# Two layer norms shared between VectorE and ScalarE, and a clamp with a second tensor in place of a constant

## The chip, the cores and the metric

The kernel runs on one NeuronCore of one Trainium2 chip. The metric is the device time of one execution in microseconds (us). The kernel before takes 867.91 us, the median of 3 runs (865.51 to 868.33).

## What is computed

Activations of 16 sequences of 256 tokens with 128 features (4096 tokens) pass through four sublayers, each on a layer norm of its input and added back to it. Cut to what matters here:

```
ln(x)   = (x - mean(x)) / sqrt(var(x) + 1e-5)                # over the 128 features
x = x + mixing(ln(x));  x = x + moe(ln(x))
x = x + attention(ln(x));  x = x + moe(ln(x))

mixing(x): Q = l2norm(x @ W_q.T); K = l2norm(x @ W_k.T); V = x @ W_v.T
           return Q * mean over the sequence of (K * V)
l2norm(t) = t / max(norm(t), 1e-12)
moe(x):    a shared 128-512-128 MLP, plus the top 2 of 8 experts of the same shape
```

The change touches the norm ahead of the mixing, the mixing's `max(norm, 1e-12)`, and the norm ahead of the first mixture of experts.

## The kernel before, in words

The tokens lie in `xres` as 32 tiles of 128 tokens (partitions) by 128 features in f32. A batch b is two tiles (one sequence); a group g is four batches, that is 8 tiles, and there are four groups. Each engine has its own instruction stream, written out by hand, and waits on semaphores.

**The first two norms** are `norm(r)`, r = 0 (ahead of the mixing) and r = 1 (ahead of the experts). VectorE merges the statistics, ScalarE takes the square root (`std`, line 1384), VectorE the reciprocal (line 1715). Then, a group at a time:
- the rows: `xn = (xres - mean) * rstd`, 8 instructions of 128x128 a group on VectorE (line 1720, `norm_rows`), mean and rstd being one value a partition
- `hi` on ScalarE (line 1391): the f16 part of the group's 128x1024 elements, into `hl`
- `lo` on VectorE (line 1727): what hi leaves over, one 128x1024 instruction that reads `xn` and `hl`
- TensorE turns both parts of each batch (line 894, four transposes) into one of four PSUM banks; when a bank has been copied out it is free for the batch four later
- the copies to `xT`: ScalarE has 12 batches (line 1395: 0 to 8, 10, 12, 14), VectorE has 9, 11, 13, 15 (line 1732), after its last `lo`

VectorE's order is rows 0, rows 1, lo 0, rows 2, lo 1, rows 3, lo 2, lo 3, copies. ScalarE's is hi 0, hi 1, copies of group 0, hi 2, copies of group 1, hi 3, the rest. In norm(1) TensorE adds the gate's eight small matmuls a batch (line 877, 128x8) when a batch is copied, and GpSimd adds each group of `xn` into `xres` (line 722) once that group's `hi` is done. The route, which VectorE works out, waits for the last gate logits.

**GpSimd meanwhile** scales and splits the weights of 8 experts and of the shared MLP (lines 690 to 698, operations of 128x512 that read SBUF), as SyncE's loads bring them, from norm(0) into the mixing; then it fills `place16` and `vx` by MEMSET (lines 707, 708) and copies into `place16` (line 712).

**Between norm(0) and the mixing** VectorE splits the biases and the transposed weights (lines 2333 to 2355); the mixing's first projection waits for that.

**The mixing** runs over the 16 batches, two PSUM banks a batch, with VectorE one batch ahead in part. For a batch TensorE projects (6 matmuls of 384 columns), ScalarE squares and sums (line 1411, four with their accumulator reads), takes the root (line 1417) and copies (line 1420). On VectorE a step is: clamp of batch b+1 (line 1748, 128x4 elements), half of `back` (line 1766), reciprocal (line 1753), the other half, `front` of b+1 (line 1759, two), statistics of b-1 (line 1694, two), the add into `xres` (line 1771, 128x256, reads two SBUF tensors).

**After norm(1)** TensorE starts the shared MLP (lines 877 and 1036) while VectorE routes.

Of the kernel before, what the change touches and what calls it, by code (L numbers as in the profile page):

```python
# [34 lines left out]
def build(nc, x, W_q, W_k, W_v, qkv_w, qkv_b, out_w, out_b, gate_w, gate_b, sh_w1, sh_b1, sh_w2,  # L35
# [50 lines left out]
    with ctx:  # L86
        def sb(name, shape, dt):
            return ctx.enter_context(nc.sbuf_tensor(name, shape, dt))

        def sem(name):  # L90
            return ctx.enter_context(nc.semaphore(name))
# [46 lines left out]
        var = sb("var", [P, T], F32)  # L138
        gap = sb("gap", [P, T], F32)
        rstd = sb("rstd", [P, T], F32)  # L140
        bnat = sb("bnat", [P, 56], F32)
        bhi = sb("bhi", [P, 56], F16)
        blo = sb("blo", [P, 56], F16)
# [137 lines left out]
        class Ln:  # L281
            stats = sem("ln_stats")
            var = sem("ln_var")
            merge = sem("ln_merge")
            std = sem("ln_std")
            rstd = sem("ln_rstd")
            norm = sem("ln_norm")
            hi = sem("ln_hi")
# [349 lines left out]
        def _(pool):  # L638
# [21 lines left out]
            pool.memset(cXS[:, :], XS)  # L660
            pool.memset(zero16[:, :], 0.0)
            pool.memset(cWS[:, :], WS)
            pool.memset(epsx[:, :], 1e-5 / (XS * XS))
            link(pool.memset(eps[:, :], 1e-5))
            for m in (ident16, ident32):
# [714 lines left out]
        def _(act):  # L1380
            def std(r):
                l, first = Ln, r * NBATCH
                act.wait_ge(l.var, r + 1)
                act.activation(rstd[:, :], var[:, :], ACT.Sqrt, bias=eps[:, 0:1], scale=1.0 / D).then_inc(l.std, 1)

            def norm(r):
                l, first = Ln, r * NBATCH

                def hi(g):
                    act.wait_ge(l.norm, NG * r + g + 1)  # L1390
                    act.activation(group(hl, g)[:, :, 0:D], group(xn, g), ACT.Copy, scale=XS).then_inc(l.hi, 1)

                def copy_out(b):
                    act.wait_ge(l.turned, first + b + 1)
                    act.activation(two(xT, b), LB[b % GB][:, 0:4 * P].rearrange("p (c f) -> p c f", c=CB),
                                   ACT.Copy).then_inc(l.xT, 1)

                for g in range(NG):
                    hi(g)
                    if 0 < g < NG - 1:  # L1400
                        for b in range(GB * (g - 1), GB * g):
                            copy_out(b)
                for b in SBATCH[2 * GB:]:
                    copy_out(b)

# [280 lines left out]
        def _(dve):  # L1686
# [14 lines left out]
            def norm(r):  # L1701
                l, first = Ln, r * NBATCH


                dve.wait_ge(l.stats, (r + 1) * NBATCH)
                dve.tensor_tensor(mean[:, :], stats[:, :, 1], stats[:, :, 4], ALU.add)
                dve.tensor_tensor(var[:, :], stats[:, :, 2], stats[:, :, 5], ALU.add)
                dve.tensor_tensor(gap[:, :], stats[:, :, 1], stats[:, :, 4], ALU.subtract).then_inc(l.merge, 1)
                dve.wait_ge(l.merge, 2 * r + 1)
                dve.tensor_scalar(mean[:, :], mean[:, :], 0.5, None, ALU.mult)  # L1710
                dve.tensor_tensor(gap[:, :], gap[:, :], gap[:, :], ALU.mult).then_inc(l.merge, 1)
                dve.wait_ge(l.merge, 2 * r + 2)
                dve.scalar_tensor_tensor(var[:, :], gap[:, :], D / 4.0, var[:, :], ALU.mult, ALU.add).then_inc(l.var, 1)
                dve.wait_ge(l.std, r + 1)
                dve.reciprocal(rstd[:, :], rstd[:, :]).then_inc(l.rstd, 1)
                dve.wait_ge(l.rstd, r + 1)

                def norm_rows(g):
                    for t in range(GT * g, GT * (g + 1)):
                        last = dve.tensor_scalar(xn[:, t, :], xres[:, t, :], mean[:, t:t + 1], rstd[:, t:t + 1],  # L1720
                                                 ALU.subtract, ALU.mult)
                    last.then_inc(l.norm, 1)

                def lo(g):
                    dve.wait_ge(l.hi, NG * r + g + 1)
                    h = group(hl, g)
                    dve.scalar_tensor_tensor(h[:, :, D:2 * D], group(xn, g), XS, h[:, :, 0:D],  # L1727
                                             ALU.mult, ALU.subtract).then_inc(l.lo, 1)

                def copy_out(b):  # L1730
                    dve.wait_ge(l.turned, first + b + 1)
                    dve.tensor_copy(two(xT, b), LB[b % GB][:, 0:4 * P].rearrange("p (c f) -> p c f", c=CB))\
                        .then_inc(l.xTv, 1)

                norm_rows(0)
                norm_rows(1)
                for g in range(2, NG):
                    lo(g - 2)
                    norm_rows(g)
                lo(NG - 2)  # L1740
                lo(NG - 1)
                for b in VBATCH:
                    copy_out(b)

            def mix():
                def clamp(b, u):
                    dve.wait_ge(Mix.std, b + 1)
                    dve.tensor_scalar(rnorm[:, u, :, :], rnorm[:, u, :, :], PS * 1e-12, None, ALU.max)\  # L1748
                        .then_inc(Mix.clamped, 1)

                def invert(b, u):
# [635 lines left out]
```

## Time and profile before

| | before |
|---|---|
| median of 3 runs | 867.91 us (865.51 to 868.33) |
| the profiled execution, its own time | 864.54 us |
| span of the profile | 862.7 us |
| TensorE matmul busy | 685.2 us (79%) |
| VectorE busy | 646.9 us (75%) |
| ScalarE busy | 526.3 us (61%) |
| GpSimd busy | 478.7 us (55%) |
| mean granted TensorE clock | 0.91 of full speed |

The shares are means over all stages. By the chain of work that ended last TensorE carries 57% of the span and VectorE 25%; among the lines of that chain are 1720 (the rows of the first two norms, 4%), 1748 (the clamp, 1%) and 1727 (`lo`, 1%). A stage's bound is read from that chain in order of time, and then from the timeline of each engine in that stretch. In the timeline a row is `start, duration, engine, line, operation, out<-in, shape, count`; a row with a count above 1 covers that many instructions from the first's start to the last's end. Instructions of one engine overlap a little at their ends, so the distance from start to start is shorter than the duration of one.

### The profile page before, as it was taken

How to read it: one execution, taken by the hardware profiler on the slowest of the kernel's cores; microseconds unless marked ns; L12 is line 12 of the kernel's file. 1: busy time of each engine (PE TensorE's matmuls, PEld its weight loads, DVE VectorE, ACT ScalarE, POOL GpSimd, SP SyncE). 2: the span in 40 equal slices, each digit the busy share in tenths (PEclk: the TensorE clock that was granted, in tenths of full speed). 3: DMA queues.
4: the chain of work that ended last, by engine and by line, in shares of the span. 5: the costliest groups of instructions: out<-in, count | busy, mean ns of one | idle time of the engine just before them, and what ended most of it. 6: DMA issues, size and time to landing. Idle time of an engine off the chain costs nothing.

```text
span 862.7 us, 22793 instructions
## 1 busy us (share of the span) xinstructions
PE 685.2 (79%) x7807; PEld 488.3 (57%) x7808; DVE 646.9 (75%) x1433; ACT 526.3 (61%) x1236; POOL 478.7 (55%) x496
## 2 busy tenths in 40 slices
PE   1265289699999906889989989997989949999980
PEld 1233289588898903334434444443438939888980
DVE  7979969477777443889989888987766228888748
ACT  3366364276676504588889788877775526666640
POOL 3987315677876277848227206003577737777740
PEclk9999569899999955699989998998899969999995
DMA  7222110033335111101000000000011322333236
GB/s 193 73 74 31 46 54 2 25 78 88 91 85 79 47 49 46 32 8 35 17 2 2 2 1 2 2 2 2 21 53 57 108 58 74 86 82 90 74 106 198
DMA packets 62745, 46.88 MB, mean 54 GB/s; under 512 B 8771, under 2 KB 57067, under 8 KB 62680
## 3 DMA queue, kind: packets, MB, share of 16 engines
q1 hardware_dynamic: 53592, 28.02, 12.1%
q0 software_dynamic: 9088, 17.98, 8.2%
q8 instruction: 42, 0.69, 0.3%
q14 instruction: 23, 0.19, 0.1%
HBM read 26.76 MB, written 20.13 MB: 54 GB/s over the span
## 4 chain that ended last, share of the span: by engine, by line
PE 57%; DVE 25%; ACT 6%; issue 5%; POOL 5%; DMA 2%; SPq 0%; DVEq 0%; ACTq 0%; POOLq 0%
PE ps L877 30%; PE ps L1021 12%; DVE mx L2226 6%; PE ps L1255 5%; DVE xn L1720 4%; PE ps L1036 3%; POOL rows L827 3%; DVE xres L2123 2%; PE ps L1113 2%; POOL gy L756 2%; PE ps L1268 1%; ACT scratch L1590 1%; DVE rnorm L1748 1%; DVE hlo L2219 1%; DVE hl L1727 1%
## 5 line engine op out<-in xcount | busy, mean ns | idle before, releaser
L1466 ACT ACTIVATE h<-ps,b1T 128x256 f32<-128x256 f32 x440 | 171.9, 479 | 56.8 <-PE ps L877 56.8
L2226 DVE TENSOR_REDUCE mx<-ps 128x2 f32<-128x512 f32 x256 | 171.9, 687 | 30.6 <-PE ps L877 29.1
L1590 ACT ACTIVATE scratch<-ps 128x512 f32<-128x512 f32 x256 | 149.4, 603 | 37.7 <-PE ps L877 36.3
L877 PE MATMUL ps<-xg,w1s 128*128 128x256 f16 x936 | 117.9, 277 | 11.4 <-issue 9.5
L1021 PE MATMUL ps<-w2s,hhi 128*128 x1248 | 117.3, 219 | 0.0
L838 POOL DMA_INDIRECT ytok<-yst,didx x78 | 89.5, 1148 | 42.9 <-DVE yst L2057 22.2
L877 PE MATMUL ps<-kst,qst 32*128 32x256 f16 x512 | 97.5, 290 | 10.6 <-DVE mx L2226 10.3
L742 POOL DMA_INDIRECT scratch<-rows,tok_i x78 | 89.9, 1153 | 26.8 <-issue 23.2
L1492 ACT ACTIVATE xg<-ps 128x512 f16<-128x512 f16 x78 | 46.5, 597 | 95.1 <-PE ps L1113 95.1
L877 PEld LDWEIGHTS ps<-xg,w1s 128*128 x936 | 88.5, 99 | 25.7 <-issue 15.5
L1999 DVE SCALAR_TENSOR_TENSOR hlo<-h,hhi 128x1024 f16<-128x1024 f32 x78 | 95.6, 1225 | 2.7
L877 PE MATMUL ps<-hlo,kst 32*128 32x256 f16 x512 | 94.5, 282 | 3.2 <-ACT scratch L1590 2.8
L1021 PEld LDWEIGHTS ps<-w2s,hhi 128*128 128x128 f16 x1248 | 86.3, 98 | 0.2
L1021 PE MATMUL ps<-w2s,hlo 128*128 x624 | 85.9, 219 | 0.0
L1255 PE MATMUL ps<-scratch,vx 128*32 128x256 f32 x1024 | 84.3, 403 | 0.3 <-ACT scratch L1590 0.3
L756 POOL DMA_INDIRECT gy<-ysorted,slot_i x64 | 61.9, 967 | 39.0 <-DMA ysorted<-yst 20.2
L827 POOL DMA_INDIRECT rows<-hl,slot_i x64 | 62.6, 978 | 19.4 <-issue 18.9
L1997 DVE TENSOR_SCALAR hhi<-h 128x1024 f16<-128x1024 f32 x78 | 54.7, 701 | 23.8 <-ACT h L1466 20.5
L1036 PE MATMUL ps<-w2f,h 128*128 128x128 f32 x512 | 63.0, 277 | 0.5 <-ACT h L1466 0.5
L773 POOL TENSOR_SCALAR yst<-xres,mean,rstd 128x128 f32<-128x128 f32 x24 | 18.7, 787 | 80.3 <-DVE rstd L2189 80.3
L2057 DVE SCALAR_TENSOR_TENSOR yst<-ps,b2s 128x256 f32<-128x256 f32 x78 | 33.1, 425 | 38.1 <-PE ps L1021 38.0
L1036 PEld LDWEIGHTS ps<-w2f,h 128*128 128x128 f32 x512 | 59.7, 192 | 1.0 <-ACT h L1466 0.7
(310 smaller groups left out, 1345.7 us busy)
## 6 DMA issues: line engine op xcount, KB each, us to landing
gy<-rows SPq DMA_DIRECT2D x39, 136.0 KB, 2.2
ysorted<-yst SPq DMA_DIRECT2D x39, 128.0 KB, 1.9
h<-in_L_ffn_ew SPq DMA_DIRECT2D x16, 256.0 KB, 3.1
scratch<-ytok SPq DMA_DIRECT2D x16, 256.0 KB, 3.4
xres<-in_L_attn_a_x SPq DMA_DIRECT2D x4, 512.0 KB, 6.1
rows<-hl SPq DMA_DIRECT2D x4, 512.0 KB, 3.3
out_x<-xres SPq DMA_DIRECT2D x4, 512.0 KB, 4.3
scratch<-rows,tok_i POOLq DMA_INDIRECT x78, 2.8
```

Of the source, the lines that this page charges most:

```text
L742: pool.indirect_dma_start(grow[:, BT * (f % 4) + t, :], None, rows_dram, bass.IndirectOffsetOnAxis(ap=tok_i[:, n:n + 1], axis=0))\
L756: pool.indirect_dma_start(gy[:, f % 4, TOPK * c + k, :], None, y_dram, bass.IndirectOffsetOnAxis(ap=slot_i[:, k, t:t + 1], axis=0))\
L827: pool.indirect_dma_start(region_dram, bass.IndirectOffsetOnAxis(ap=slot_i[:, k, t:t + 1], axis=0), hl[:, t, :], None).then_inc(Post.sent, 16)
L838: pool.indirect_dma_start(ytok_dram, bass.IndirectOffsetOnAxis(ap=didx[:, u, t:t + 1], axis=0), yst[:, u, t, :], None, bounds_check=most, ...
L877: return pe.matmul(o, a, b, start=start, stop=stop)
L1021: last = pe.matmul(YB[u % 2][:, t, :], h[:, u % 2, at:at + P], w, start=(c, k, t) == (0, 0, 0), stop=(c, k, t) == (CH - 1, 2, BT - 1), ski ...
L1036: pe.matmul(YB[q % 2][:, t, :], h32[:, q % 2, at:at + P], w2f[:, c * D:(c + 1) * D], start=(c, t) == (0, 0), stop=False, skip_group_check= ...
L1255: last = pe.matmul(ps[32 * hh:32 * hh + 32, 4 + jp, n * SEQ:(n + 1) * SEQ], vx[:, u, kc, 4 * (2 * jp + n) + hh, :], prb[:, (4 * g + hh) % ...
L1466: last = act.activation(h32[:, u % 2, f], HB[u % 2][:, f], ACT.Gelu_apprx_tanh, bias=b1T[:, ds(e * CH + c, 1)], scale=1.0 / PS)
L1590: act.activation(prb[:, (s // 4 * 4 + (s + 2) % 4) % 8, :], ps[:, s % 2, :], ACT.Exp, scale=HD ** -0.5 / (PS * PS))\
L1999: dve.scalar_tensor_tensor(hlo[:, u, :], h32[:, u, :], XS, hhi[:, u, :], ALU.mult, ALU.subtract)\
L2226: dve.tensor_reduce(mx[:, c, j:j + 5:4], ps[:, 2 + s % 2, :].rearrange("p (n k) -> p n k", n=2), AX_X, ALU.max).then_inc(Att.mx, 1)
```

## The change

In norm(0) and norm(1):
- VectorE makes one more small vector, `shift = -mean * rstd` (128x32).
- The rows of groups 1 and 3 move to ScalarE: `Identity(rstd * x + shift)`, 8 instructions a group, both operands one value a partition. ScalarE's order becomes rows 1, hi 0, hi 1, rows 3, hi 2, copies of group 0, hi 3, copies of group 1, the rest.
- The rows of groups 0 and 2 stay on VectorE, as SCALAR_TENSOR_TENSOR in place of TENSOR_SCALAR: `rstd` is given as a second tensor, one column read 128 times. VectorE's order becomes rows 0, rows 2, lo 0, lo 1, lo 2, lo 3, copies.
- The semaphore `std` becomes `by_act` and counts three steps a norm.

In the mixing the clamp reads its bound from a constant tensor `least` (128x2x2, filled once by GpSimd at the start) as TENSOR_TENSOR, in place of a constant in TENSOR_SCALAR.

```diff
@@ vector, norm(r)
-                dve.wait_ge(l.std, r + 1)
+                dve.wait_ge(l.by_act, 3 * r + 1)
                 dve.reciprocal(rstd[:, :], rstd[:, :]).then_inc(l.rstd, 1)
-                dve.wait_ge(l.rstd, r + 1)
+                dve.wait_ge(l.rstd, 2 * r + 1)
+                dve.scalar_tensor_tensor(shift[:, :], mean[:, :], -1.0, rstd[:, :], ALU.mult, ALU.mult)\
+                    .then_inc(l.rstd, 1)
 
                 def norm_rows(g):
                     for t in range(GT * g, GT * (g + 1)):
-                        last = dve.tensor_scalar(xn[:, t, :], xres[:, t, :], mean[:, t:t + 1], rstd[:, t:t + 1],
-                                                 ALU.subtract, ALU.mult)
+                        last = dve.scalar_tensor_tensor(xn[:, t, :], xres[:, t, :], mean[:, t:t + 1],
+                                                        rstd[:, t:t + 1].to_broadcast([P, D]),
+                                                        ALU.subtract, ALU.mult)
                     last.then_inc(l.norm, 1)
...
                 norm_rows(0)
-                norm_rows(1)
-                for g in range(2, NG):
-                    lo(g - 2)
-                    norm_rows(g)
-                lo(NG - 2)
-                lo(NG - 1)
+                norm_rows(2)
+                for g in range(NG):
+                    lo(g)
                 for b in VBATCH:
                     copy_out(b)
@@ vector, mix()
-                    dve.tensor_scalar(rnorm[:, u, :, :], rnorm[:, u, :, :], PS * 1e-12, None, ALU.max)\
+                    dve.tensor_tensor(rnorm[:, u, :, :], rnorm[:, u, :, :], least[:, :, :], ALU.max)\
                         .then_inc(Mix.clamped, 1)
@@ scalar, norm(r)
+                def scaled_rows(g):
+                    act.wait_ge(l.rstd, 2 * r + 2)
+                    for t in range(GT * g, GT * (g + 1)):
+                        last = act.activation(xn[:, t, :], xres[:, t, :], ACT.Identity, bias=shift[:, t:t + 1],
+                                              scale=rstd[:, t:t + 1])
+                    last.then_inc(l.by_act, 1)
+
                 def hi(g):
-                    act.wait_ge(l.norm, NG * r + g + 1)
+                    if g % 2:
+                        act.wait_ge(l.by_act, 3 * r + g // 2 + 2)
+                    else:
+                        act.wait_ge(l.norm, 2 * r + g // 2 + 1)
                     act.activation(group(hl, g)[:, :, 0:D], group(xn, g), ACT.Copy, scale=XS).then_inc(l.hi, 1)
...
-                for g in range(NG):
+                scaled_rows(1)
+                hi(0)
+                hi(1)
+                scaled_rows(3)
+                for g in range(2, NG):
                     hi(g)
-                    if 0 < g < NG - 1:
-                        for b in range(GB * (g - 1), GB * g):
-                            copy_out(b)
+                    for b in range(GB * (g - 2), GB * (g - 1)):
+                        copy_out(b)
```

## Rows read from the trace of the kernel before

**Rows 1.** Chain of waits in order of time, norm(0): start, us, what.
```profile
13.86 4.19 DVE xn L1720 x16
...
19.19 6.54 DVE xn L1720 x8
...
34.93 3.59 PE ps L894 x32
```

**Rows 2.** Chain of waits, from the mixing to the experts.
```profile
77.82 2.92 DVE rnorm L1748
...
92.77 6.29 DVE xn L1720 x16
...
110.78 0.59 PE ps L894 x4
...
115.84 5.71 PE ps L877 x64
```

**Rows 3.** Timeline of norm(0): GpSimd's first weights, and VectorE's `lo` among them.
```profile
18.92 2.16 POOL L690 TENSOR_TENSOR h<-h,cWS 128x512 f32<-128x512 f32 x2 [13.17 <-DMA h<-in_L_ffn_ew]
25.65 2.07 DVE L1727 SCALAR_TENSOR_TENSOR hl<-xn,hl 128x1024 f16<-128x1024 f32 x1
26.59 1.60 POOL L694 CAST w1s<-h 128x512 f32 x1
```

**Rows 4.** Timeline of ScalarE, norm(0) and later: what its row instruction is priced by.
```profile
15.44 0.23 ACT L1672 ACTIVATE gws<-scratch 128x8 f16<-128x8 f32 x1
16.04 1.06 ACT L1391 ACTIVATE hl<-xn 128x1024 f16<-128x1024 f32 x1 [0.36 <-DVE xn L1720]
19.89 2.06 ACT L1395 ACTIVATE xT<-ps 128x512 f16<-128x512 f16 x4 [0.74 <-PE ps L894]
92.03 0.32 ACT L1384 ACTIVATE rstd<-var,eps 128x32 f32<-128x32 f32 x1 [4.62 <-DVE var L1713]
115.86 1.28 ACT L1458 ACT_TABLE_LOAD   x1
201.04 1.56 ACT L1466 ACTIVATE h<-ps,b1T 128x256 f32<-128x256 f32 x4
```

**Rows 5.** Timeline: VectorE's STT of 128x128 from SBUF; a tiny two-tensor operation.
```profile
854.84 4.27 DVE L2123 SCALAR_TENSOR_TENSOR xres<-scratch,wtop,xres 128x128 f32<-128x128 f32 x15
128.44 0.17 DVE L1978 TENSOR_TENSOR e<-e,e 128x8 f32<-128x8 f32 x1
```

**Rows 6.** Timeline of the mixing: clamps and adds beside GpSimd.
```profile
53.07 0.41 DVE L1771 TENSOR_TENSOR xres<-xres,scratch 128x256 f32<-128x256 f32 x1
53.14 0.81 POOL L694 CAST w2s<-h 128x512 f32 x1
53.39 0.58 DVE L1748 TENSOR_SCALAR rnorm<-rnorm 128x4 f32<-128x4 f32 x1
77.16 1.80 POOL L707 MEMSET place<- 128x2048 f16 x1
82.33 0.29 DVE L1748 TENSOR_SCALAR rnorm<-rnorm 128x4 f32<-128x4 f32 x1
```

**Rows 7.** Two lines of VectorE, all instructions: duration ns least/median/most, first and last start.
```profile
L1748 DVE TENSOR_SCALAR rnorm<-rnorm x16: 155/575/2984, 46.3 to 87.0; 128x4 f32<-128x4 f32 x16
L1771 DVE TENSOR_TENSOR xres<-xres,scratch x16: 399/409/1048, 49.7 to 90.0; 128x256 f32 x12, 128x256 f32<-128x256 f32 x4
```

**Rows 8.** Timeline of norm(1): GpSimd's first and last add, and the `lo` beside it.
```profile
96.08 2.38 POOL L722 TENSOR_TENSOR xres<-xres,xn 128x1024 f32<-128x1024 f32 x1 [13.49 <-ACT hl L1391]
109.42 2.43 DVE L1727 SCALAR_TENSOR_TENSOR hl<-xn,hl 128x1024 f16<-128x1024 f32 x2
110.67 3.39 POOL L722 TENSOR_TENSOR xres<-xres,xn 128x1024 f32<-128x1024 f32 x1 [2.79 <-ACT hl L1391]
```

**Rows 9.** Stretches: length, busy PE, PEld, DVE, ACT, POOL, granted clock, DMA share, GB/s.
```profile
116.00:120.00 4.00, 4.00 (x50) 3.06 (x48) 3.18 (x8) 3.27 (x5) 0.00 (x0) 0.50 0.03 7
122.00:126.00 4.00, 4.00 (x40) 3.87 (x39) 1.95 (x4) 2.30 (x8) 0.00 (x0) 1.00 0.00 0
```

More of the change, by code:

```diff
@@ L140, in build @@
         rstd = sb("rstd", [P, T], F32)
+        shift = sb("shift", [P, T], F32)
+        least = sb("least", [P, CB, 2], F32)
         bnat = sb("bnat", [P, 56], F32)
@@ L284, in build @@
             merge = sem("ln_merge")
-            std = sem("ln_std")
+            by_act = sem("ln_by_act")
             rstd = sem("ln_rstd")
@@ L662, in _ @@
             pool.memset(cWS[:, :], WS)
+            pool.memset(least[:, :, :], PS * 1e-12)
             pool.memset(epsx[:, :], 1e-5 / (XS * XS))
@@ L1383, in std @@
                 act.wait_ge(l.var, r + 1)
-                act.activation(rstd[:, :], var[:, :], ACT.Sqrt, bias=eps[:, 0:1], scale=1.0 / D).then_inc(l.std, 1)
+                act.activation(rstd[:, :], var[:, :], ACT.Sqrt, bias=eps[:, 0:1], scale=1.0 / D).then_inc(l.by_act, 1)
             def norm(r):
                 l, first = Ln, r * NBATCH
+                def scaled_rows(g):
[4 more added lines that the diff above has]
+                    last.then_inc(l.by_act, 1)
                 def hi(g):
-                    act.wait_ge(l.norm, NG * r + g + 1)
+                    if g % 2:
+                        act.wait_ge(l.by_act, 3 * r + g // 2 + 2)
+                    else:
+                        act.wait_ge(l.norm, 2 * r + g // 2 + 1)
                     act.activation(group(hl, g)[:, :, 0:D], group(xn, g), ACT.Copy, scale=XS).then_inc(l.hi, 1)
```

## The prediction

> **What bounds the kernel now.** I read the chain of work that ended last in order of time, then each engine's timeline in the stretches that the change touches. In norm(0) the chain is VectorE's rows and `lo` from 13.86, then TensorE's turns from 34.93 to 38.52 [rows 1]. The reader should compare the row stretches: 16 rows take 4.19 us, but the 8 rows of group 2 take 6.54 [rows 1]. The difference is GpSimd, which starts on the weights at 18.92 [rows 3]. From then on VectorE and GpSimd take turns: `lo` starts at 25.65 and takes 2.07, where half of two later ones is 1.21 [rows 8], and GpSimd's cast, queued at 26.59, takes 1.60 because `lo` runs first [rows 3]. In the mixing, clamps of 128x4 elements take a median of 575 ns where the shortest takes 155 [rows 7]; one sits 2.92 us on the chain, just behind the start of GpSimd's MEMSETs [rows 2, 6]. norm(1) is bound by VectorE again, from 92.77 until TensorE's last unbroken run begins at 110.78; the stage ends at 115.84 [rows 2]. So all three places are on the path, and what is saved there moves everything behind it: the shared MLP on TensorE, and the route, which waits for the gate logits. The expert weights don't come in between: GpSimd is past them at 77.16 [rows 6], 38 us before they are used.
>
> **Prices.** (a) A row on VectorE as SCALAR_TENSOR_TENSOR: 15 of the same form (128x128, one pointer, two tensors in SBUF) take 4.27 us [rows 5], so they start about 0.28 us apart. The old form takes 4.19/16 = 0.26 [rows 1]. VectorE loses 0.02 a row on 32 rows and is rid of the other 32.
> (b) A row on ScalarE: no row of the trace has two pointers. From SBUF, 1024 elements take 1.06 and 32 elements with a pointer 0.32; four of 256 elements with a pointer take 1.56, so they are at most 0.39 apart [rows 4]. Half the elements take off 0.11 (0.83 ns each: 1.06 us less some 0.2 fixed, over 1024). A second pointer adds about 0.09: the 0.32 less 0.03 for its elements, less the 0.2. That gives 0.37; I take 0.375 apart. Bounds: 0.28 (as if pointers were free) and 0.49 (0.2 + 0.11 + two pointers, with no overlap).
> The Trainium skill, "ScalarE: Activation LUTs", section "What ACT_TABLE_LOAD costs", has 186 ns + 0.833 ns an element, about 93 ns for each pointer and an overlap of about 93 ns: an estimate of 0.386 apart, by which norm(0) would end 0.2 us later.
> (c) `shift` lies between 0.17 (128x8) and 0.28 (128x128) [rows 5]; 0.2 in norm(1). In norm(0) it is hidden behind ScalarE's weight copies, which end at 15.67 [rows 4].
> (d) The clamp with two tensors: 0.17 us by the nearest row [rows 5], against 0.155. What it waits for is the question. The add of line 1771 also has two tensors in SBUF: it takes 0.40 at least and up to 1.05 [rows 7]. So a two-tensor operation is held up too when GpSimd reads SBUF. At 53.07 the add goes first, GpSimd's cast queues behind it (to 53.95), and the next clamp queues behind the cast (0.58, to 53.97) [rows 6]. Nothing in that depends on the clamp's form. I take as gone only the wait behind the MEMSETs, which read nothing.
> The Trainium skill has this as a rule ("SBUF — State Buffer", "Who interferes with whom"): an instruction with two SBUF inputs contends with a GpSimd instruction that reads SBUF, not with one that only writes. The trace agrees for the add (up to 1.05); for a MEMSET beside a two-tensor operation it has no row. Against the change speaks "VectorE: DVE Perf Modes" of the skill: f32 TENSOR_SCALAR has twice the rate of a two-tensor form, an estimate of 32x128/0.96 GHz/2 = 2.1 us lost; the rows show 32x0.02 = 0.6.
>
> **norm(0), step by step.** VectorE: `shift`, then 16 rows from 14.0, done at 14.0+16x0.28 = 18.5, before GpSimd starts at 18.92 [rows 3]; no row is held up any more. ScalarE is now the bound. From 15.6: rows 1 take 8x0.375+0.1 = 3.1, to 18.7; hi 0 and hi 1, 0.95 apart, to 20.6; rows 3 to 23.6; hi 2 to 24.6; four copies (four take 2.06, [rows 4]) to 26.5; hi 3 to 27.45; four copies to 29.4. Beside it the four `lo` each wait for the GpSimd operation under way (0.6 to 1.1) and then take 1.14: done at about 21.1, 23.3, 26.7 and 29.0, none later than ScalarE needs it. The turns of batches 8 to 11 follow the copies of 4 to 7 (28.0 to 29.9), the last four follow the copies of 8 to 11, about 0.45 apart, and end at 31.8. Before they ended at 38.52 [rows 1]. Gain 6.7. At 0.28 or 0.49 a row the chain moves by 16 times the difference: 8.2 or 4.9.
> VectorE's splits of biases and weights follow; I leave their length as it was. GpSimd is held up about 1.1 us by each `lo`, four instead of three: it ends some 1.2 later, hidden by the 38 us above.
>
> **The mixing.** It starts 6.7 earlier, and GpSimd's weights end 1.2 later. The MEMSET wait of 2.8 goes. But beside GpSimd the clamps come (77.8-46.3)/12 = 2.62 us apart [rows 2, 7]; from there to the last, at 87.0 [rows 7], three steps take 9.2, or 6.4 without that wait. These now lie beside GpSimd's weights too: 3x2.62 = 7.9. Net gain 2.8-1.5 = 1.3; bounds 0 (the clamp waits for the MEMSETs all the same, or lands in other waits) and 2.8.
>
> **norm(1)**, in us from the first row; GpSimd is idle at first. VectorE's 16 rows end at 16x0.28+0.07 = 4.55. ScalarE's rows 1 end at 3.2, hi 0 at 4.2. That frees GpSimd's add of group 0 (2.38, [rows 8]) beside VectorE's last row, and lo 0. Before, hi 3 freed lo 3 and the last add together: `lo` went first and the add took 3.39 [rows 8]. From then on the two alternate, 1.15+2.4 = 3.55 a group: if lo 0 starts at 4.55, lo 3 ends at 4.55+3x3.55+1.15 = 16.35; if the add goes first, at about 18.7. Before, lo 3 ended at 109.42+2.43-92.77 = 19.1 [rows 8, 2], but what set the end, 115.84-92.77 = 23.1, was lo 2 and the eight turns with gates behind it, 5.06. Now it is lo 3 and four turns with gates: some 3.3, so 19.7 or 22.0. Gain 3.4 or 1.1.
> What is late next is TensorE's clock: it is granted 0.50 in 116 to 120 and 1.00 in 122 to 126 [rows 9], that is 1.2 and 2.4 GHz, after an unbroken run from 110.78. The new unbroken run begins only behind lo 3 (16.4 or 18.8, before 18.0), so some 2 us more of the MLP run at half speed: cost 1.0. Net 2.4 or 0.1. The ends of hi 0 and of VectorE's rows lie 0.35 apart, too near to call; I take 1.1.
>
> **Sum.** 6.7 + 1.3 + 1.1 = 9.1 us. The profiled execution would go from 864.54 to 855.4. It lies 3.4 below the median of the runs shown; the median would go from 867.91 to 858.8. All bounds low: 4.9+0+0.1 = 5.0; all high: 8.2+2.8+2.4 = 13.4. The runs before scatter by 1.4 around their middle.
>
> **Rivals.** 1. *Two-tensor operations are not held up by GpSimd's reads.* Then all clamps come as near as the last ones, (87.0-82.33)/2 = 2.33 [rows 6, 7]: 15x2.33 = 35.0 for 40.7, gain 5.7 in the mixing. norm(1) loses its alternation, follows ScalarE and ends near 17.6: 4.5 after the clock's cost. In all 6.7+5.7+4.5 = 16.9, 851.0. For it: the median add takes 0.409, though GpSimd is busy most of that time. Against: the 1.05. Chance 0.12.
> 2. *The waits for GpSimd fall badly*: its adds go first in norm(1), and four VectorE operations more on the path (splits, adds, `lo`) arrive just behind a GpSimd one and wait 1.0 each. Gain 6.7+0.1+1.3-4.0 = 4.1, 863.8; with more such waits down to 1. For it: at 96.08 the add took its plain 2.38 while VectorE was in its rows [rows 8], so it gets in between any two. Against: VectorE's rows no longer lie in GpSimd's way. Chance 0.14.
> 3. *ScalarE's rows are far dearer.* The place is ScalarE's queue in both norms; 0.1 us a row costs 1.6 in norm(0), and 1.6 in norm(1) once the 4.4 us are used up by which hi 3 (11.95) leads the end of lo 3. The 9.1 are gone at 0.375+(9.1+4.4)/32 = 0.80 a row; at 1.0 the kernel would be 6.4 slower, 874.3. A function table loaded (1.28, [rows 4]) at each change to Identity and back would cost up to six loads, 7.7 us: 866.5. Against: 256 elements with a pointer stay below 0.39 apart, and in the mixing Square, Sqrt and Copy alternate without a load. Chance 0.06, of it 0.04 slower than before.
> The Trainium skill ("ScalarE: Activation LUTs", "Table sets: the hidden batching unit") has copy and identity in every set; no row here has Identity.
>
> **How the numbers follow.** Forecast (gain 5.0 to 13.4) 0.68; rivals 0.12, 0.14, 0.06. The range takes in the forecast's bounds with the scatter (853.1 to 864.3) and so part of rival 2: 853.0 to 864.5. A measurement of this kernel can tell about 0.3%, 2.6 us, from no change. Faster by more: 0.91 (forecast, rival 1, most of rival 2); within: 0.05 (the rest of rival 2, rival 3's loads); slower: 0.04.
>
> **What would show it.** norm(0): no row of VectorE longer than 0.35; ScalarE without a gap from 15.6 to 29, its rows 0.375 apart; the last turn near 31.8, the mixing's first matmul near 36. Mixing: clamps still near 0.57 beside reading GpSimd, none near 2.9. norm(1): whether lo 0 or add 0 starts first, lo 3 ending 16.35 or 18.7 from the first row, the clock's rise 27 to 29 from it. Wrong would be: ScalarE's rows above 0.49, a table load between them, or clamps all near 0.17.

## The result, and the profile after

| | before | after |
|---|---|---|
| median, runs taken side by side | 868.12 us (865.51 to 868.59) | 857.37 us (854.40 to 857.90) |
| profiled execution, its span | 864.54, 862.7 | 857.65, 855.8 |

The ratio is 0.987, 95% interval 0.983 to 0.991: faster by 10.8 us between the medians, and the interval stands for 7.5 to 15 us. The two profiled executions lie only 6.9 apart; where the other 3.9 are is told below. The page of after:

```profile
span 855.8 us, 22796 instructions
PE 688.5 (80%) x7807; PEld 487.9 (57%) x7808; DVE 632.7 (74%) x1403; ACT 537.4 (63%) x1268; POOL 483.5 (56%) x497
PE 57%; DVE 21%; ACT 7%; POOL 6%; issue 5%; DMA 2%; SPq 1%; DVEq 0%; ACTq 0%; POOLq 0%
```

Four marks divide the part that the change touches: the end of the last turn of norm(0), the first matmul of the mixing, the reciprocal of norm(1), and matmul 390, one of the last 40 matmuls of the gates, just ahead of the shared MLP. From the same marks of both traces:

| us from the span's start | before | after | stage shorter by |
|---|---|---|---|
| last turn of norm(0) ends | 38.50 | 32.03 | 6.5 |
| mixing's first matmul | 42.78 | 37.03 | -0.7 |
| norm(1)'s reciprocal | 92.38 | 86.47 | 0.2 |
| matmul 390 | 115.84 | 105.00 | 4.9 |

The sum is 10.8, and 10.7 of it still stand at matmul 2470 (295.34 before, 284.64 after).

**norm(0)** in the chain of waits of after (start, us, what), where [rows 1] had VectorE's rows:

```profile
15.86 3.05 ACT xn L1395 x8
18.91 1.89 ACT hl L1404 x2
20.80 3.08 ACT xn L1395 x8
...
28.22 3.82 PE ps L897 x32
...
32.41 0.91 DVE bhi L2349
...
33.40 1.02 DVE blo L2353
...
34.48 0.94 DVE qkb L2359
```

ScalarE has taken VectorE's place on the chain. The last three lines are the splits of biases behind the norm: operations on three and two columns that take about 1 us each, because GpSimd holds them off (the first two end within 0.03 us of the end of one of its operations). In before the same three took 0.40, 0.91 and 1.01: two of them were held off there already. All instructions of the two row lines (duration ns least/median/most, first and last start):

```profile
L1395 ACT ACTIVATE xn<-xres,shift,rstd x32: 477/492/511, 15.7 to 94.8; 128x128 f32<-128x128 f32 x32
L1738 DVE SCALAR_TENSOR_TENSOR xn<-xres,mean,rstd x32: 343/344/348, 14.0 to 90.9; 128x128 f32<-128x128 f32 x32
```

**The mixing.** Clamps and adds of after, where [rows 7] had 155/575/2984 and 399/409/1048, and the clamp that met a MEMSET, where [rows 2] had 2.92:

```profile
L1764 DVE TENSOR_TENSOR rnorm<-rnorm,least x16: 151/562/1111, 40.6 to 81.0; 128x4 f32<-128x4 f32 x16
L1787 DVE TENSOR_TENSOR xres<-xres,scratch x16: 401/748/1236, 43.7 to 84.1; 128x256 f32 x12, 128x256 f32<-128x256 f32 x4
...
75.84 1.80 POOL L710 MEMSET place<- 128x2048 f16 x1
76.43 0.15 DVE L1764 TENSOR_TENSOR rnorm<-rnorm,least 128x4 f32<-128x4 f32 x1
```

The long wait is gone, the typical clamp is as slow as it was, and the adds have become slower (the median from 409 to 748 ns).

**norm(1)**: the timeline of VectorE and GpSimd in after, where [rows 8] had the last `lo` and the last add beside each other:

```profile
86.97 4.28 DVE L1738 SCALAR_TENSOR_TENSOR xn<-xres,mean,rstd 128x128 f32<-128x128 f32 x16
91.25 4.52 DVE L1746 SCALAR_TENSOR_TENSOR hl<-xn,hl 128x1024 f16<-128x1024 f32 x2
91.30 13.26 POOL L725 TENSOR_TENSOR xres<-xres,xn 128x1024 f32<-128x1024 f32 x4 [10.03 <-ACT hl L1404]
96.22 6.12 DVE L1746 SCALAR_TENSOR_TENSOR hl<-xn,hl 128x1024 f16<-128x1024 f32 x2 [0.46 <-ACT hl L1404]
```

`lo` 0 started 0.05 us ahead of the first add. From there the two take turns to 102.34. But in the chain of waits of the stage it is ScalarE's queue that leads, to the end of its last `hi`, and VectorE has only the last `lo` in it:

```profile
87.08 3.19 ACT xn L1395 x8
...
98.11 0.95 ACT hl L1404
99.09 3.27 DVE hl L1746
...
102.49 0.59 PE ps L897 x4
```

**Where 3.9 us went.** Behind matmul 2470 the profiled execution of after gives back what the medians keep. The stretches of before and then of after (length, busy PE, PEld, DVE, ACT, POOL, granted clock, DMA share, GB/s):

```profile
590.00:625.00 35.00, 32.16 (x342) 14.52 (x341) 25.76 (x60) 26.30 (x54) 17.43 (x25) 0.85 0.04 11
```

```profile
590.00:625.00 35.00, 34.52 (x354) 14.86 (x354) 25.21 (x57) 24.18 (x51) 19.08 (x26) 0.76 0.07 22
```

TensorE's clock is at 0.50 for 17.1 us from 590.0 in after, for 10.2 us from 598.8 in before. The lead falls there from 9.57 us (matmul 5200) to 7.07 (matmul 5590); another 1.2 went between matmuls 2470 and 3120, where after has one more stretch at 0.50, 3.4 us from 364.7. Nothing of the change lies there, and the profiled execution of before (864.54) was quicker than all four of its timed runs (865.51 and more), while that of after (857.65) was a typical one. So I put the 3.9 down to which executions were profiled; that is argued from these rows, not shown by a run.

### The profile page after: what moved, and what is told of

It is laid out like the page before. It is cut to its first block, busy times and chain, and to the rows that moved or that the text cites. A ratio compares the mean times of both kernels' runs of the same rounds, so it can differ in the third digit from the quotient of the medians.

```text
span 855.8 us, 22796 instructions
## 1 busy us (share of the span) xinstructions
PE 688.5 (80%) x7807; PEld 487.9 (57%) x7808; DVE 632.7 (74%) x1403; ACT 537.4 (63%) x1268; POOL 483.5 (56%) x497
## 3 DMA queue, kind: packets, MB, share of 16 engines
q0 software_dynamic: 9088, 17.98, 8.3%
## 4 chain that ended last, share of the span: by engine, by line
PE 57%; DVE 21%; ACT 7%; POOL 6%; issue 5%; DMA 2%; SPq 1%; DVEq 0%; ACTq 0%; POOLq 0%
PE ps L880 30%; PE ps L1024 12%; DVE mx L2242 6%; PE ps L1258 6%; PE ps L1039 3%; POOL rows L830 3%; DVE xres L2139 2%; PE ps L1116 2%; POOL gy L759 2%; PE ps L1271 2%; ACT xn L1395 1%; DVE hlo L2235 1%; DVE rnorm L1764 1%; DVE xres L1787 1%; ACT hl L1404 1%
## 5 line engine op out<-in xcount | busy, mean ns | idle before, releaser
L745 POOL DMA_INDIRECT scratch<-rows,tok_i x78 | 91.7, 1175 | 26.8 <-issue 19.8
L1258 PE MATMUL ps<-scratch,vx 128*32 128x256 f32 x1024 | 86.8, 413 | 0.3 <-ACT scratch L1606 0.3
```

The costliest lines, as they stand in the source:

```text
L745: pool.indirect_dma_start(grow[:, BT * (f % 4) + t, :], None, rows_dram, bass.IndirectOffsetOnAxis(ap=tok_i[:, n:n + 1], axis=0))\
L1258: last = pe.matmul(ps[32 * hh:32 * hh + 32, 4 + jp, n * SEQ:(n + 1) * SEQ], vx[:, u, kc, 4 * (2 * jp + n) + hh, :], prb[:, (4 * g + hh) % ...
```

## The experiments

Times are compared with the kernel before on the same chip. Where e5 to e11 were run, every kernel, the one before too, took some 110 to 125 us more. In the trace of after from there (the row "after, again") all of that lies behind the first 160 us, and what it is stays open. So the marks are read across, and ratios only within a comparison. "Mixing" is the time from the mixing's first matmul to the reciprocal, "norm(1)" the time from there to matmul 390 (counted from 0).

The marks come from one profiled execution of each kernel, and they move with the way GpSimd's and VectorE's streams happen to fall: e3 has the mixing of before, unchanged, and it takes 3.8 us more there (53.39 against 49.60). The ratios are no finer than their intervals, which are 0.6 to 1.9% wide. Those of e2, e4, e5 and e7 to e10 overlap with that of after. What these runs show is read from the marks and from the durations of single operations.

| kernel | norm(0) ends | mixing starts | reciprocal | matmul 390 | mixing | norm(1) | ratio to before |
|---|---|---|---|---|---|---|---|
| before | 38.50 | 42.78 | 92.38 | 115.84 | 49.60 | 23.46 | 1 |
| after | 32.03 | 37.03 | 86.47 | 105.00 | 49.44 | 18.53 | 0.987 |
| after, again | 31.83 | 36.69 | 85.80 | 104.33 | 49.11 | 18.53 | 0.9895 |
| e1 | 39.56 | 44.20 | 92.08 | 115.54 | 47.88 | 23.46 | 0.9965 |
| e2 | 31.85 | 36.94 | 90.12 | 108.64 | 53.18 | 18.52 | 0.9874 |
| e3 | 39.34 | 43.61 | 97.00 | 120.76 | 53.39 | 23.76 | 1.0014 |
| e4 | 31.88 | 36.88 | 87.97 | 106.50 | 51.09 | 18.53 | 0.9896 |
| e5 | 31.79 | 36.93 | 81.20 | 99.72 | 44.27 | 18.52 | 0.9838 |
| e6 | 38.11 | 42.52 | 91.24 | 115.26 | 48.72 | 24.02 | one run |
| e7 | 31.85 | 36.85 | 86.66 | 104.83 | 49.81 | 18.17 | 0.9894 |
| e8 | 32.05 | 32.66 | 85.53 | 104.05 | 52.87 | 18.52 | 0.9819 |
| e9 | 31.84 | 32.45 | 79.90 | 97.88 | 47.45 | 17.98 | 0.981 |
| e10 | 38.69 | 42.96 | 85.89 | 109.35 | 42.93 | 23.46 | 0.9883 |
| e11 | 31.70 | 32.31 | 77.66 | 95.87 | 45.35 | 18.21 | 0.9781 |

**e1: the clamp alone**, in the kernel before.

```diff
-                    dve.tensor_scalar(rnorm[:, u, :, :], rnorm[:, u, :, :], PS * 1e-12, None, ALU.max)\
+                    dve.tensor_tensor(rnorm[:, u, :, :], rnorm[:, u, :, :], least[:, :, :], ALU.max)\
```

> The kernel before with the clamp alone changed to the two-tensor maximum; norms as before. Theory (two-tensor operations wait for GpSimd's reads, not for its MEMSETs): the clamp at the MEMSETs drops from 2.98 to about 0.15, the others stay near a median of 0.57; the first rows of norm(1) start 2.8 earlier than 92.77, near 90.0, and the whole is 2.8 us faster (ratio 0.997). Rival (the wait moves on into the adds, which also have two tensors): 0 to 1 us faster. Rival (tiny two-tensor operations are free of the port): median near 0.17, rows start near 87, 5 to 6 us faster.

Median 866.02 against 870.69 us, ratio 0.9965 (0.9934 to 0.9996). All clamps of e1:

```profile
L1750 DVE TENSOR_TENSOR rnorm<-rnorm,least x16: 150/178/995, 47.7 to 86.7; 128x4 f32<-128x4 f32 x16
```

No clamp is near 2.98, as expected. But the mixing is 1.7 us shorter, not 2.8, and the reciprocal comes only 0.3 earlier than in before: in this execution norm(0) ended 1.1 later, with VectorE's last 8 rows beside GpSimd taking 6.18 us where before took 5.15, though no edit touches them. The median clamp fell to 178 ns, where after has 562 with the same instruction. So how much a small operation waits for GpSimd's reads depends on how the two streams happen to fall, not on its form alone. What the clamp is worth by itself is not settled: 0.3 us at the marks, 0.3 to 5.7 by the ratio's interval.

**e2: the norms alone**: after, with the old clamp. **e4: only which engine has which rows**: as e2, and VectorE's rows in the old form. **e3: only the form**: before, with VectorE's rows in the new form.

```diff
-                        last = dve.tensor_scalar(xn[:, t, :], xres[:, t, :], mean[:, t:t + 1], rstd[:, t:t + 1],
-                                                 ALU.subtract, ALU.mult)
+                        last = dve.scalar_tensor_tensor(xn[:, t, :], xres[:, t, :], mean[:, t:t + 1],
+                                                        rstd[:, t:t + 1].to_broadcast([P, D]),
+                                                        ALU.subtract, ALU.mult)
```

> The changed kernel with the old clamp (constant in TENSOR_SCALAR). Theory: norm(0) and norm(1) as in the changed kernel (last turn of norm(0) near 32.0, norm(1) 18.9 from first row to last gate matmul), but one clamp of some 2.9 behind the MEMSETs, so the rows of norm(1) start near 89.8 instead of 86.97: 2.8 us slower than the changed kernel, 8 us faster than before (0.991). Rival (the clamp's form is worth nothing, the phase decides): equal to the changed kernel within 1 us.

> The kernel before with its rows as SCALAR_TENSOR_TENSOR, all 32 a norm still on VectorE in the old order, clamp old. Theory (the two-tensor form is held up by GpSimd's reads like the old one, only the move helps): rows of group 2 still 6 to 7 us for 8, last turn of norm(0) within 1 us of 38.5, rows 0.28 apart where undisturbed; 0 to 1.5 us slower than before. Rival (the form is what frees the rows): the 8 rows of groups 2 and 3 take 2.3 each, norm(0) 5 to 7 us shorter.

> The changed kernel with the old forms on VectorE (rows of groups 0 and 2 as TENSOR_SCALAR, old clamp): the move to ScalarE alone. Theory (the 16 rows lie before GpSimd's start, so their form doesn't matter in norm(0); in norm(1) hi 0 still comes near the end of VectorE's rows): norm(0)'s last turn near 32.0, norm(1) 18.9 from first row to last gate matmul, the whole within 1 us of the kernel with the new norms and the old clamp, 8 us faster than before. Rival (form decides in norm(1)): GpSimd's first add gets in between the TENSOR_SCALAR rows or before lo 0 and norm(1) is 2.4 longer.

Medians 858.68 (0.9808 to 0.994), 870.73 (0.9985 to 1.0043) and 860.82 (0.9865 to 0.9928). norm(0) and norm(1) are the same in e2, e4 and after to 0.2 us: the whole gain of the norms is the move to ScalarE, and the form of the rows left on VectorE is worth nothing. In e3 the two groups of 8 rows beside GpSimd take 6.24 and 6.28, where the old form took 6.63 and 5.15 by the same view; the new form waits for a reading GpSimd just as well. Two misses: e2 reaches matmul 390 3.6 us behind after, where 2.8 was expected, but its ratio is that of after; and e3 reaches it 4.9 us behind before, where at most 1.5 was expected, but its ratio is 1.0014, for which no run gives a reason.

These three still have the one-tensor clamp, and each shows what it does at the MEMSETs. Timelines of e3, then of e4 (GpSimd's MEMSETs and the clamp that met them):

```profile
74.25 4.60 DVE L1749 TENSOR_SCALAR rnorm<-rnorm 128x4 f32<-128x4 f32 x1
...
75.29 1.80 POOL L707 MEMSET place<- 128x2048 f16 x1
77.03 1.80 POOL L708 MEMSET vx<- 128x2048 f32 x1
```

```profile
79.10 1.80 POOL L711 MEMSET vx<- 128x2048 f32 x1
79.15 1.77 DVE L1763 TENSOR_SCALAR rnorm<-rnorm 128x4 f32<-128x4 f32 x1
```

In e3 the clamp first waits for a reading operation of GpSimd (to 75.35), then ends at 78.85, with the second MEMSET (78.83): two MEMSETs back to back go ahead of it, as they did in before (77.74 to 80.73). In e4 it met only the second. Between 1.58 (e2) and 4.60 us is luck of the phase. With two tensors six clamps fell inside a MEMSET (two each in after, e1 and e6), and all took 0.15 to 0.16. That part of the prediction is shown. The mixing of e2 and e4 is 53.18 and 51.09, with the new clamp 49.44.

**e5: no second operand in SBUF**: after, with the clamp's constant and the mixing's products in PSUM (the constant is written there by one small VectorE MEMSET ahead of the mixing). **e10: the same in before.**

```diff
-                    dve.tensor_tensor(rnorm[:, u, :, :], rnorm[:, u, :, :], least[:, :, :], ALU.max)\
+                    dve.tensor_tensor(rnorm[:, u, :, :], rnorm[:, u, :, :], LEAST, ALU.max)\
...
+        LEAST = ps[:, 6, 2 * D:2 * D + 2 * CB].rearrange("p (c j) -> p c j", c=CB)
+        def QG(u):
+            return ps[:, 6 + u, 0:CB * D].rearrange("p (c d) -> p c d", c=CB)
```

> The changed kernel, but the clamp's bound and the products that the mixing adds into xres lie in PSUM, so that neither the clamp nor the add has two tensors in SBUF. Theory (what still slows the mixing is the port shared with GpSimd's reads, reached by the second SBUF tensor): all clamps near 0.16 to 0.2 and all adds near 0.40 to 0.45 beside busy GpSimd; the mixing goes at 2.3 us a batch throughout, 43 to 45 us from its first matmul to norm(1)'s reciprocal instead of 49.4, and the whole is 5 us faster than the changed kernel (ratio to the kernel before near 0.982). Rival (the waits are pacing, not the port: they would move to TensorE or ScalarE): mixing within 1 us of 49.4.

> The kernel before with the clamp's bound and the products in PSUM, norms as before: the mixing free of GpSimd, but starting late (42.8). Theory: the mixing takes the same 44.3 us from its first matmul to norm(1)'s reciprocal as with the new norms, so its 49.6 before held 5.3 of waits for GpSimd (2.8 of them at the MEMSETs), and the changed kernel's 49.4 holds 5.1 (none at the MEMSETs): its earlier start bought as much more waiting for reads as the clamp's new form saved. The whole 5.3 us faster than before (0.994). Rival (an early mixing is slower for another reason than the port): 42 or less here.

e5: 979.72 against 995.05 us, ratio 0.9838 (0.9742 to 0.9933). e10: 971.31 against 983.72, ratio 0.9883 (0.9837 to 0.9929). The clamps and adds of e5:

```profile
L1773 DVE TENSOR_TENSOR rnorm<-rnorm,ps x16: 157/158/159, 40.6 to 74.5; 128x4 f32<-128x4 f32 x16
L1796 DVE TENSOR_TENSOR xres<-xres,ps x16: 400/403/410, 43.6 to 77.6; 128x256 f32 x12, 128x256 f32<-128x256 f32 x4
```

No clamp and no add waits any more, with GpSimd as busy as before. A clamp comes every (74.5-40.6)/15 = 2.26 us, in after every (81.0-40.6)/15 = 2.69. One operation of e5 does still wait, at the end of the mixing, where the statistics are merged. The halving of the mean has one tensor, as the old clamp had, and here it met GpSimd's second MEMSET:

```profile
78.74 1.80 POOL L716 MEMSET vx<- 128x2048 f32 x1
79.02 1.56 DVE L1731 TENSOR_SCALAR mean<-mean 128x32 f32<-128x32 f32 x1
```

It takes 0.18 in before, after and e10. Less these 1.4 us the mixing of e5 is 42.9, as that of e10 (42.93), though the one starts 6 us ahead of the other. So the waits for GpSimd are 6.7 of the 49.60 us of before and 6.5 of the 49.44 of after. Of the 6.7 the MEMSETs made 2.8 (the clamp's 2.98 less 0.16), which leaves 3.9 for reads; in after no operation of the mixing waited at a MEMSET, so all 6.5 are reads. This is where the change's gain in the mixing went: the mixing starts earlier, so more of it lies beside GpSimd's weights, and what the clamp no longer loses to MEMSETs it and its neighbours lose to reads.

e10, with none of the change in it, is 6.5 us ahead of before at matmul 390, where the change is 10.8 ahead. It was expected to take 44.3 for the mixing and to be 5.3 faster as a whole (0.994); the 44.3 had the wait of the halving in it, and the 12.4 us between the medians are more than the 6.5 at the marks. Where the rest came from is open.

**e6: does ScalarE set the norms' length?** After, with each of ScalarE's rows computed a second time into a spare tensor (work added, nothing left out).

```diff
+                        act.activation(scratch[:, ds(D * (t - GT - GT * (g // 2)), D)], xres[:, t, :], ACT.Identity, bias=shift[:, t:t + 1],
+                                              scale=rstd[:, t:t + 1])
```

> The changed kernel with every row of ScalarE computed twice (the extra result goes to a scratch tile that nobody reads): the price of ScalarE's queue. Theory (ScalarE bounds norm(0), but has slack in norm(1)): norm(0)'s last turn 16x0.375 = 6.0 later, near 38.0; norm(1) only 2 to 4 longer than its 18.5 from reciprocal to first MLP matmul, since hi 3 ends 3.3 before lo 3 in the changed kernel. Rival (VectorE's lo operations and GpSimd bound norm(0) too): less than 4 later there.

One run, 994.22 us. norm(0) ends at 38.11, 6.1 later: 16 rows by 0.385, ScalarE alone sets its length. norm(1) grew by 5.5, more than the 2 to 4 that I expected. I had given ScalarE 4.4 us of slack there; at most 0.7 is left.

**e7: GpSimd's adds behind the last `lo`**, in after.

```diff
-                    pool.wait_ge(l.hi, NG + g + 1)
+                    pool.wait_ge(l.lo, 2 * NG)
```

> The changed kernel, but GpSimd's four adds of norm(1) wait until the last lo is done instead of each for its hi. Theory (the lo operations no longer alternate with the adds, so each takes 1.2 instead of 2.2 to 3.4; then TensorE's eight turns with gates, freed by ScalarE's copies from 98.9 on, are the bound): from reciprocal to first MLP matmul 17.5 to 18 instead of 18.53, 0.5 to 1 us faster in all. Rival (the alternation is the bound, as the prediction had it): 2 us or more shorter. Rival (the adds come late for the first shared result): nothing gained, or slower.

983.33 us, ratio 0.9894 (0.9816 to 0.9971), no different from that of after there. norm(1) is 18.17 instead of 18.53. VectorE's timeline in e7:

```profile
91.44 2.36 DVE L1746 SCALAR_TENSOR_TENSOR hl<-xn,hl 128x1024 f16<-128x1024 f32 x2
96.41 1.22 DVE L1746 SCALAR_TENSOR_TENSOR hl<-xn,hl 128x1024 f16<-128x1024 f32 x1 [2.61 <-ACT hl L1404]
99.28 1.23 DVE L1746 SCALAR_TENSOR_TENSOR hl<-xn,hl 128x1024 f16<-128x1024 f32 x1 [1.64 <-ACT hl L1404]
```

Without adds VectorE waits for ScalarE's `hi` twice, and `lo` 3 ends at 100.51, 13.9 from the reciprocal where it was 15.9. Of these 2.0 us the stage keeps 0.4. TensorE's stretches in e7, first column behind the length:

```profile
100.00:101.00 1.00, 1.00 (x21) 1.00 (x20) 0.50 (x1) 1.00 (x3) 0.42 (x1) 0.50 0.43 112
101.00:102.00 1.00, 1.00 (x25) 1.00 (x23) 0.42 (x1) 0.94 (x3) 1.00 (x1) 0.50 0.54 158
102.00:103.00 1.00, 1.00 (x23) 1.00 (x22) 0.42 (x1) 0.32 (x2) 1.00 (x2) 0.50 0.99 288
```

From 99.8 on TensorE is busy without a gap: its turns with gates are the bound now, and they begin when ScalarE's queue lets them. With e6 this settles norm(1): the taking of turns by `lo` and the adds, on which the prediction built the stage's length, is worth 0.4 us there, and ScalarE's queue sets the rest.

**e8: the splits of biases behind norm(0) moved ahead of `lo` 0**, in after, where they are done before GpSimd is busy.

```diff
+            def splits():
...
                 norm_rows(2)
+                if r == 0:
+                    splits()
                 for g in range(NG):
                     lo(g)
```

> The changed kernel, but VectorE's splits of biases and weights, which lie between norm(0)'s last copy and the mixing (4.6 us, three of them near 1.0 behind GpSimd), are moved into VectorE's gap behind its rows, at 18.3, mostly before GpSimd starts at 19.2. Theory: the splits take about 2.4 us there, lo 0 ends near 22 instead of 21.1 and is still hidden behind ScalarE; the mixing's first matmul comes at about 32.8 instead of 37.0, and the whole is 3 to 4.5 us faster. Rival (the late lo 0 and the fuller VectorE delay the turns): the last turn of norm(0) 1 to 2 us later and half of the gain lost.

980.67 us, ratio 0.9819 (0.9744 to 0.9893). The mixing starts 4.4 earlier (32.66), and of that 0.9 is left at the reciprocal, where 3 to 4.5 was expected for the whole. The adds, all 16 together (busy us, mean ns, idle before), in after, in e8, and in e9, where their second operand is in PSUM:

```profile
L1787 DVE TENSOR_TENSOR xres<-xres,scratch 128x256 f32 (+1 forms) x16 | 11.0, 686 | 0.0
```

```profile
L1817 DVE TENSOR_TENSOR xres<-xres,scratch 128x256 f32 (+1 forms) x16 | 12.0, 748 | 0.0
```

```profile
L1826 DVE TENSOR_TENSOR xres<-xres,ps 128x256 f32 (+1 forms) x16 | 6.5, 406 | 0.0
```

e8 is the change's own story once more: an earlier mixing runs beside more of GpSimd's weights and is held off more (52.87 against 49.44 us). The adds are busy 1.0 us longer of these 3.4; most of the rest stands as the clamps' waits for ScalarE's root, 7.0 us in all where after has 5.1. That all of it goes back to the operands' place is shown by e9: there the mixing takes 41.6 us to its last statistics, as it does in e5, which starts it 4.5 later.

**e9: e5, e7 and e8 together.**

> The changed kernel with the three edits together: splits early, clamp bound and products in PSUM, GpSimd's adds after the last lo. Theory (the time that the early splits gained was given back in the mixing, which then lay longer beside GpSimd's reads; with no second SBUF tensor it can't be): first matmul of the mixing near 32.7, 44.3 us to norm(1)'s reciprocal, at 77.0 instead of 86.5, 18.2 from there to the MLP's first matmul, at 95.2 instead of 105.0: 9.8 us faster than the changed kernel, 0.976 of the kernel before. Rival (something else lengthens an early mixing, the loads of the weights for one): reciprocal at 80 or later.

968.77 against 983.72 us, ratio 0.981 (0.9762 to 0.9857). The mixing starts at 32.45 and its last statistics end at 74.0. But the reciprocal comes at 79.90, where the 44.3 of e5 would have given 77.0, and 42.9, without the wait that e5 has in it, 75.4. VectorE's timeline, with GpSimd's MEMSET:

```profile
75.70 1.80 POOL L715 MEMSET place<- 128x2048 f16 x1
75.86 3.42 DVE L1759 TENSOR_SCALAR mean<-mean 128x32 f32<-128x32 f32 x1
```

The halving now lies under both MEMSETs; in before it came 10 us behind them, in e5 it met the second. It makes 3.2 of the 4.5 us between 75.4 and 79.90. The rest is in two of the merge's two-tensor operations beside GpSimd's reads (0.60 and 1.18 us, where before has 0.22 for each). So the rival "80 or later" was all but met, and the cause is the same trap, in the next place.

**e11: e9 with the halving as a two-tensor operation.**

```diff
-                dve.tensor_scalar(mean[:, :], mean[:, :], 0.5, None, ALU.mult)
+                dve.scalar_tensor_tensor(mean[:, :], mean[:, :], -0.5, mean[:, :], ALU.mult, ALU.add)
```

> This is e9_all with one more edit: in norm() the halving of the mean is written as a two-tensor operation (mean, -0.5, mean) on VectorE instead of an operation with a scalar on one tensor. Theory (an operation that reads one tensor is held off as long as GpSimd has a MEMSET under way or next, one that reads two tensors is not): in e9_all the halving waited 3.42 us at 75.86; here it takes about 0.2 there, norm(1)'s reciprocal starts near 76.5 instead of 79.90, matmul 390 near 94.5 instead of 97.88, and the run is about 3.4 us faster than e9_all: a ratio to the kernel before near 0.977. Rival (the wait belongs to the place and not to the form: another small operation of the merge takes it over): the reciprocal at 79 or later, matmul 390 at 97 or later, and the ratio that of e9_all, 0.981.

957.81 against 980.14 us, ratio 0.9781 (0.9718 to 0.9843). The reciprocal starts at 77.66, 2.2 earlier than in e9, short of the 76.5. VectorE's and GpSimd's timeline in e11:

```profile
75.54 0.49 DVE L1759 SCALAR_TENSOR_TENSOR mean<-mean 128x32 f32<-128x32 f32 x1
...
76.17 1.10 DVE L1762 SCALAR_TENSOR_TENSOR var<-gap,var 128x32 f32<-128x32 f32 x1
...
77.16 1.80 POOL L715 MEMSET place<- 128x2048 f16 x1
...
78.16 2.97 DVE L1771 SCALAR_TENSOR_TENSOR xn<-xres,mean,rstd 128x128 f32<-128x128 f32 x11
```

The test is less clean than it was meant to be: GpSimd came to its MEMSETs 1.46 us later than in e9, so the halving never met them, and it can't be said from this run what it would have cost under them. 1.1 of the 2.2 us lie ahead of the merge (statistics done at 72.9 instead of 74.0), and the edit has no part in them: the mixing's first 12 matmuls start 0.16 us apart here and 0.32 in e9. Within the merge the 3.42 are gone, but three of its two-tensor operations took 1.07 to 1.10 beside GpSimd's reads. So half of the rival came true as well: other operations of the merge took over most of the wait, and only 1.1 us are left of the 3.2. What the run does show is that the 11 rows from 78.16, two tensors each, run at 0.27 apart inside the MEMSETs. e11 is the fastest version of this study. Its interval lies below that of after in the same sort of session (0.9895, 0.9855 to 0.9935).

## Why the prediction was right, and where its steps were wrong

The forecast was 9.1 us, the medians give 10.8 and the traces 10.8 at matmul 390. That the sum came out near is luck in part: the mixing and the splits gave 1.8 less than forecast, norm(1) gave 3.8 more.

- **norm(0), forecast 6.7, measured 6.5.** Every step held: ScalarE's rows 0.385 apart (3.08/8; I took 0.375), no row on VectorE above 0.348, the last turn at 32.03 (31.8). The estimate of 0.386 from the Trainium skill, "ScalarE: Activation LUTs", section "What ACT_TABLE_LOAD costs", agrees with the 0.385. There was no table load between Sqrt, Identity and Copy in either norm, so that part of rival 3 falls.
- **The splits behind it, taken as unchanged, cost 0.7 more.** Three of them take 0.91, 1.02 and 1.01 us beside GpSimd's weights; in before the first of them took 0.40 (the others 0.91 and 1.01). I had listed GpSimd's extra lateness as hidden by 38 us and not asked who else it would hold off. (There was no such lateness: it came to its MEMSETs at 75.84, in before at 77.16.)
- **The mixing, forecast 1.3, measured 0.2.** The long wait went, as priced (2.8): 0.15 us under a MEMSET. The loss from lying longer beside GpSimd was sized at 1.5 and was 2.6 (2.8 less the 0.2 that is left); with the old clamp kept, e4 lost 1.5 and e2 3.6. That term rested on the distance of clamps in before, 2.62 us, where adds were mostly free (409 ns); in after they wait too (748 ns). The mixing started 5.75 us earlier and GpSimd reached its MEMSETs 1.3 earlier, so the two lay beside each other 4.4 us longer. e5 and e10 show that the difference is waiting and nothing else: without the second operands' waits, and less the 1.4 us of the halving, both mixings take 42.9, so reads cost 3.9 us in before and 6.5 in after, 2.6 more.
- **norm(1), forecast 1.1, measured 4.9.** The path was wrong. The prediction let `lo` and GpSimd's adds, taking turns, set the end, with 4.4 us of slack for ScalarE. e7 takes the turns away and the stage loses 0.4; e6 doubles ScalarE's rows and the stage grows by 5.5 of the 6.2 added. So ScalarE's queue sets the end, with 0.7 of slack at most. The sizes were off too. The case that I called too near to call went the good way (`lo` 0 at 91.25, the add at 91.30), whose net was forecast at 2.4; the 1.1 that I took is neither that nor the 0.1 of the bad case, and the prediction gives no reason for it. From 2.4: I read 115.84 as the end of the stage, but that row [rows 2] is the start of a run of 64 matmuls whose first 40 are the last gates, and the MLP's first is at 116.75 (in after 105.90), 0.9 more. `lo` 3 ended 15.4 us from the first row, not 16.35, 1.0 more. The four turns with gates behind it took 3.56, not 3.3, 0.3 less. And the clock's cost of 1.0 was not there. That makes 5.0 from the first row; `shift` takes 0.1 of it. Stretches of after, where [rows 9] had 0.50 up to 120:

```profile
99.00:100.00 1.00, 0.85 (x16) 0.77 (x14) 0.96 (x2) 1.00 (x4) 1.00 (x1) 0.50 0.01 2
100.00:101.00 1.00, 1.00 (x24) 1.00 (x23) 1.00 (x1) 1.00 (x4) 1.00 (x1) 0.50 1.00 296
...
102.00:103.00 1.00, 0.82 (x18) 0.76 (x16) 1.00 (x3) 0.11 (x1) 1.00 (x1) 0.50 0.06 17
...
109.00:110.00 1.00, 1.00 (x10) 0.69 (x7) 0.93 (x3) 1.00 (x4) 0.00 (x0) 1.00 0.00 0
```

  The clock rose from 0.50 (1.2 GHz) to 1.00 (2.4 GHz) at 108.7, 21.7 us from the first row; I had forecast 27 to 29, from an unbroken run that begins behind `lo` 3 (102.49). But TensorE was at work from 96.7 already, with turns that need no `lo` 3, and paused only for 0.15 us ahead of 99.6 and for 0.18 ahead of 102.49. In before it had stood idle from 108.25 to 110.78, worked on from there without a pause, and the clock rose at 120.9. Which of these things moved the rise, no run shows. The lead is 10.85 at matmul 390 and 10.86 at matmul 520: the clock cost nothing.
- **The rivals.** Rival 1 (no waits beside reads) is refuted by the 562 and 748 ns and by e5. Rival 2 (adds first in norm(1), more waits) happened in part: more waits came in the splits and in the mixing's adds, but in norm(1) `lo` 0 went first. Rival 3 needed rows above 0.49; they took 0.385.

## What to carry to other kernels

Where two engines hold each other off, as VectorE and GpSimd do here, a gain on one moves its work beside more of the other's: before adding up stage gains, count which operations will newly lie beside the busy engine (e8 won 4.4 us and kept 0.9). Taking the second operand out of SBUF removed the waits of the clamps and the adds altogether (e5, e10), where changing the form of the operation removed only those behind MEMSETs. A TENSOR_SCALAR on one tensor that is harmless today is a trap for the next shift of the schedule (e5, e9). Giving it a second tensor in SBUF is not a full cure: beside GpSimd's reads such operations still took 1.1 us each (e11).

## What the runs showed that I had not expected

- A VectorE operation of four columns that reads one tensor took 4.60 us, 1.1 of them behind a reading operation and the rest behind two MEMSETs of 1.80 back to back (e3): it did not get in between them there, nor in before. The Trainium skill, "SBUF — State Buffer", section "Who interferes with whom", has it that a VectorE instruction with two SBUF inputs contends with a GpSimd instruction that reads SBUF and not with one that only writes it; the trace of after agrees for the MEMSET too, with 0.15 us.
- It is not every operation on one tensor that waits so: the reciprocal of the same four columns (RECIPROCAL, line 1769) fell inside the MEMSETs of after twice, and all 16 took 0.16 to 0.18 us. Clamp and halving, which did wait, are TENSOR_SCALAR.
- The same clamp has a median of 178 ns in e1 and 562 in after, beside the same GpSimd instructions.
- With one operand in PSUM the clamps vary by 2 ns (157 to 159) beside GpSimd's reads.
- Writing the second row operand as a broadcast column costs VectorE nothing that shows: 16 rows in 4.28 us against 4.19.
